# First-layer silu as one ScalarE activation, two more scan pairs on GpSimd, and retimed steps

## The reference, cut to what matters

```python
# x: (16, 512, 256), INNER = 512 channels, 16 states
xx, res = split(x @ in_w.T)                     # 512 channels each
xx = silu(conv4(xx) + conv_b)
delta, B, C = split(xx @ xproj_w.T)             # 16, 16, 16
delta = softplus(delta @ dt_w.T + dt_b)
h[l] = exp(delta[l] * A) * h[l-1] + delta[l] * B[l] * xx[l]    # per channel and state
y[l] = sum over states of h[l] * C[l], + xx * D
x1 = layernorm(x + (y * silu(res)) @ out_w.T)
h = silu((x1 @ w1.T) * w1_s) * ((x1 @ w2.T) * w2_s)            # 1024 wide: the first layer
h = gelu((h @ h1.T) * h1_s)
h = gelu((h @ h2.T) * h2_s)
out = layernorm(x1 + (h @ w3.T) * w3_s)
```

## Time and profile before

| | us |
|---|---|
| median of three runs | 2681.95 (2679.81 to 2683.85) |
| the profiled execution | 2681.34 |
| its span, first to last instruction | 2679.5 |

### The profile page before, as it was taken

The page is one execution under the profiler, slowest core; times in us unless marked ns, Lnnn a source line. Parts: engine busy times, 40 slices in busy tenths (PEclk is TensorE's granted clock), DMA queues, the critical chain, the costliest instruction groups (busy, mean ns, idle before and its releaser), DMA issues. The chain is left out here.

```text
span 2679.5 us, 36236 instructions
## 1 busy us (share of the span) xinstructions
PE 2423.5 (90%) x12098; PEld 1844.0 (69%) x12098; DVE 2413.4 (90%) x2388; ACT 2101.1 (78%) x3225; POOL 1605.8 (60%) x1561
## 2 busy tenths in 40 slices
PE   5677999989999998989999899998989899898988
PEld 2445776867767686776767677686767768576777
DVE  6899999999999999999999999999999999999730
ACT  5886988969788896978879697887969789696611
POOL 1335567665756666566566656656665675657554
PEclk7889999999999999999999999999999999999999
DMA  7758999989899898989989898998989899898933
GB/s 250 217 138 197 223 216 223 228 211 237 206 225 225 214 231 209 238 204 223 223 219 232 206 236 200 228 224 213 243 205 229 204 231 223 212 241 201 254 105 114
DMA packets 224491, 573.26 MB, mean 214 GB/s; under 512 B 25664, under 2 KB 26048, under 8 KB 223824
## 3 DMA queue, kind: packets, MB, share of 16 engines
q0 software_dynamic: 71424, 260.08, 51.9%
q1 hardware_dynamic: 152880, 310.84, 35.3%
HBM read 301.86 MB, written 20.45 MB: 120 GB/s over the span
## 5 line engine op out<-in xcount | busy, mean ns | idle before, releaser
L792 DVE TENSOR_TENSOR_SCAN scan_ps<-dA,scan_ps 128x1024 f32<-128x1024 f32 x411 | 939.7, 2286 | 62.4 <-PE scan_ps L420 61.5
L1001 POOL DMA_DIRECT2D y<-hC x496 | 441.6, 890 | 714.8 <-DVE hC L803 544.6
L651 ACT ACTIVATE dB<-duT,bT 128x512 f32<-128x512 f32 x1024 | 711.0, 712 | 50.9 <-PE scan_ps L420 50.8
L539 PE MATMUL ffn_ps<-hb_hi,ring 128*128 128x512 f32 x1536 | 655.2, 427 | 36.5 <-DVE gate L908 17.4
L642 ACT ACTIVATE dA<-delta,ch 128x512 f32<-128x512 f32 (+1 forms) x1024 | 681.3, 711 | 0.9
L420 PE MATMUL scan_ps<-ident,dB 128*128 128x128 f32 x4096 | 556.7, 282 | 76.8 <-DVE hC L803 60.9
L420 PEld LDWEIGHTS scan_ps<-ident,dB 128*128 128x128 f32 x4096 | 488.1, 145 | 193.7 <-issue 67.2
L539 PE MATMUL ffn_ps<-hb_lo,ring 128*128 128x512 f32 x1536 | 611.2, 398 | 0.0
L803 DVE TENSOR_TENSOR hC<-scan_ps,c_rows_sb 128x1024 f32<-128x1024 f32 x411 | 501.0, 1219 | 42.6 <-DMA c_rows_sb<-c_rows 5.7
L539 PE MATMUL ffn_ps<-ha_hi,ring 128*128 128x512 f32 x1024 | 428.0, 418 | 25.9 <-POOL ha_lo L1042 25.7
L539 PE MATMUL ffn_ps<-ha_lo,ring 128*128 128x512 f32 x1024 | 402.5, 393 | 0.0
(11 more groups left out here) (103 smaller groups left out, 3172.2 us busy)
## 6 DMA issues: line engine op xcount, KB each, us to landing
y<-hC POOLq DMA_DIRECT2D x496, 512.0 KB, 6.3
ring<-rounded_weights SPq DMA_DIRECT2D x704, 256.0 KB, 4.9
c_rows_sb<-c_rows SPq DMA_DIRECT2D x256, 256.0 KB, 5.0
x<-ffn_w SPq DMA_DIRECT2D x22, 512.0 KB, 6.1
rounded_weights<-ffn_w SPq DMA_DIRECT2D x22, 512.0 KB, 6.4
xt<-x_chan SPq DMA_DIRECT2D x16, 512.0 KB, 3.9
xt<-x_tok SPq DMA_DIRECT2D x16, 512.0 KB, 5.5
out_st<-x_chan SPq DMA_DIRECT2D x16, 512.0 KB, 4.9
```

Source lines behind the costliest of these rows:

```text
L539: mm = nc.tensor.matmul(dst, w, a, start=(first and n == 0), stop=(last and n == len(steps) - 1))
L651: nc.scalar.activation(dB[:, n % 2, t, :], duT[:, t, :], ACT.Copy, scale=bT2[:, par, t, n:n + 1]).then_inc(dB_ready, 1)
L792: nc.vector.tensor_tensor_scan(states, dA[:, a:a + 2, :].rearrange("p a l -> p (a l)"), b, 0.0, ALU.mult, ALU.add).then_inc(scan_done, 1)
L1001: pool.dma_start(y2[:, par, c:c + 2, :], hC[:, slot], accum_op=ALU.add).then_inc(y_added[p % 2], 16)
```

## The change

The first layer's activation becomes one Silu on ScalarE with the full scale; VectorE's gate operation goes, and so do the two operations at the start that halved the scales. A PSUM buffer with a first product is now released by ScalarE's silu and no longer by VectorE's gate. Two more pairs of rows 1 to 15, 7 and 10, get their product on GpSimd. Some steps of the tail, the end, the transposes, the first and second layer, the front and the exponentials are a step or two (at most four) earlier or later, and the output's store is issued at step 26 and no longer 24.

```diff
-T_RES = (0, 6, 7, 9)
-T_GATE = (2, 5, 8, 11)
-T_OUT = (12, 14, 16, 17)
+T_RES = (0, 5, 7, 9)
+T_GATE = (2, 5, 8, 10)
+T_OUT = (13, 14, 15, 16)
-E_W3 = (10, 11, 12, 18)
-E_SCALE = (12, 19)
-E_ADD = (14, 20)
-E_STATS = (17, 21)
+E_W3 = (10, 12, 13, 18)
+E_SCALE = (13, 19)
+E_ADD = (15, 20)
+E_STATS = (15, 21)
-L1_AT = (22, 24, 25, 26, 27, 28, 29, 31)
+L1_AT = (23, 24, 25, 26, 27, 28, 30, 31)
-EXP_COUNT = (1, 2, 0, 0, 2, 0, 3, 1, 0, 1, 0, 0, 0, 3, 1, 0, 0, 4, 0, 1, 3, 0, 0, 1, 2, 0, 2, 1, 0, 0, 2, 0, 1, 2,
-             1, 0, 2, 3, 1, 0, 2, 1, 3, 0, 1, 0, 0, 0, 3, 2, 0, 0, 0, 2, 3, 0, 0, 0, 1, 0, 0, 2, 3, 1)
+EXP_COUNT = (0, 3, 0, 0, 2, 0, 1, 2, 2, 0, 0, 2, 1, 2, 1, 0, 0, 0, 2, 1, 4, 0, 0, 0, 3, 1, 0, 1, 0, 2, 1, 0, 1, 0,
+             3, 0, 3, 1, 2, 0, 2, 1, 2, 1, 0, 0, 0, 0, 0, 5, 0, 0, 0, 1, 4, 0, 0, 0, 2, 0, 2, 0, 0, 3)
...
-OUT_AT = 24
+OUT_AT = 26
-POOL_PAIRS = (1, 8, 11, 13, 16, 17)
+POOL_PAIRS = (1, 7, 8, 10, 11, 13, 16, 17)
...
-                        pe.wait_ge(l1_x32 if prev % 2 else l1_gate, f * HC + (prev // 2 + 1))
+                        pe.wait_ge(l1_x32 if prev % 2 else l1_silu, f * HC + (prev // 2 + 1))
...
-                    nc.scalar.activation(gate[:, o % 2, :], ffn_ps[2 * o % 3][:], ACT.Tanh,
-                                         scale=s1_half[:, o:o + 1]).then_inc(l1_tanh, 1)
+                    nc.scalar.activation(gate[:, o % 2, :], ffn_ps[2 * o % 3][:], ACT.Silu,
+                                         scale=fs[:, 0, o:o + 1]).then_inc(l1_silu, 1)
...
-                nc.vector.tensor_scalar(s1_half, s1_half, 0.5, None, ALU.mult).then_inc(const_dve, 1)
...
-                nc.vector.tensor_tensor(s12_half, s1_half, s12_half, ALU.mult).then_inc(const_s12, 1)
...
             def l1_tile(f, o):
-                dve.wait_ge(l1_tanh, f * HC + (o + 1))
-                nc.vector.scalar_tensor_tensor(out=gate[:, o % 2, :], in0=gate[:, o % 2, :], scalar=1.0,
-                                               in1=ffn_ps[2 * o % 3][:], op0=ALU.add, op1=ALU.mult
-                                               ).then_inc(l1_gate, 1)
-                dve.wait_ge(l1_gate, f * HC + (o + 1))
+                dve.wait_ge(l1_silu, f * HC + (o + 1))
                 dve.wait_ge(pe_l1, f * (2 * HC) + (2 * o + 2))
                 if o >= X32:
                     dve.wait_ge(ffn_lo, f * FFN_TILES + (o - X32 + 1))
                 nc.vector.scalar_tensor_tensor(out=x32[:, o % X32, :], in0=gate[:, o % 2, :],
-                                               scalar=s12_half[:, o:o + 1], in1=ffn_ps[(2 * o + 1) % 3][:],
+                                               scalar=fs[:, 1, o:o + 1], in1=ffn_ps[(2 * o + 1) % 3][:],
```

More of the change, by code:

```diff
@@ L47 @@
 T_X1T = (20, 21)
-E_W3 = (10, 11, 12, 18)
-E_SCALE = (12, 19)
-E_ADD = (14, 20)
-E_STATS = (17, 21)
+E_W3 = (10, 12, 13, 18)
+E_SCALE = (13, 19)
+E_ADD = (15, 20)
+E_STATS = (15, 21)
 E_NORM = 22
-B_AT = (-2, 0, 4, 5, 7, 9, 10, 12, 14, 15, 18, 20, 22, 24, 26, 28, 31, 32, 34, 35, 37, 40, 42, 43, 47, 48, 50, 51,
+B_AT = (-2, 0, 3, 5, 7, 8, 10, 12, 14, 15, 18, 20, 22, 25, 26, 28, 31, 32, 34, 35, 37, 40, 41, 42, 47, 48, 50, 51,
         54, 56, 58, 61)
-L1_AT = (22, 24, 25, 26, 27, 28, 29, 31)
+L1_AT = (23, 24, 25, 26, 27, 28, 30, 31)
 L1_SPLIT_AT = (22, 24, 25, 26, 27, 28, 29, 30)
[L57 to L60, removed]
+HALF_AT = (31, 32, 34, 35, 36, 37, 38, 40, 41, 44, 45, 46, 47, 48, 49, 50, 51, 52, 53, 54, 55, 56, 57, 59, 61, 62,
+           63, 66, 67, 70, 71, 72)
+GELU_AT = (38, 39, 39, 45, 47, 47, 49, 50, 56, 57, 57, 65, 65, 66, 72, 73)
+SPLIT_AT = (38, 40, 40, 48, 48, 50, 51, 51, 57, 58, 63, 66, 68, 70, 71, 72)
 F_XX = (30, 32, 34, 36)
@@ L65 @@
 F_BT = 48
[L66 to L75, removed]
+F_BT_OUT = 49
+F_DT = (40, 41, 43, 47)
+F_PLUS = (42, 45, 46, 49)
+F_BASE = (41, 44, 45, 49)
+F_LOST = (45, 47, 49, 51)
+F_LN = 52
+F_DELTA = (54, 54, 54, 54)
+F_DELTA_U = (54, 54, 54, 54)
+F_Y = (55, 56, 60, 62)
+F_DU = (55, 56, 57, 59)
 F_XR = 51
@@ L175, in build @@
         conv_half, a_neg = ch[:, :, 0:TAPS + 1], ch[:, :, C_ALOG:]
-        s1_half, s12_half = fs[:, 0, :], fs[:, 1, :]
         xT_front = xt[:].rearrange("p (k t) d -> p k (t d)", k=KD)
@@ L216, in build @@
         const_conv, const_dve = sem("const_conv"), sem("const_dve")
-        const_exp, const_s12 = sem("const_exp"), sem("const_s12")
+        const_exp = sem("const_exp")
         low_seen_dve, low_seen_act = sem("low_seen_dve"), sem("low_seen_act")
@@ L245, in build @@
         ln_rstd = [sem(f"ln_rstd{i}") for i in range(2)]
-        l1_tanh, l1_gate, l1_x32 = sem("l1_tanh"), sem("l1_gate"), sem("l1_x32")
+        l1_silu, l1_x32 = sem("l1_silu"), sem("l1_x32")
         gelu_x32, ffn_hi, ffn_lo = sem("gelu_x32"), sem("ffn_hi"), sem("ffn_lo")
@@ L252, in build @@
         block = ctx.enter_context(nc.Block())
-        CONST_LOADS, CONST_DVE = 6, 7
+        CONST_LOADS, CONST_DVE = 6, 6
         FFN_TILES = 3 * HC
@@ L775, in scale_constants @@
                                         ).then_inc(const_dve, 1)
-                nc.vector.tensor_scalar(s1_half, s1_half, 0.5, None, ALU.mult).then_inc(const_dve, 1)
                 dve.wait_ge(const_exp, 1)
                 nc.vector.tensor_scalar(a_neg, a_neg, -1.0, None, ALU.mult).then_inc(const_dve, 1)
-                dve.wait_ge(const_dve, CONST_DVE)
-                nc.vector.tensor_tensor(s12_half, s1_half, s12_half, ALU.mult).then_inc(const_s12, 1)
             def scan_pair(r, p):
```

## The result

The changed kernel takes 2754.3 us (median of four runs, 2752.2 to 2755.3) beside 2680.9 for the kernel before: a ratio of 1.0272, with an interval of 1.0259 to 1.0285. It is 73 us slower; 2688 was forecast, in a range that ended at 2745.

The account below looks back on a forecast made before the run. Each row was taken as some 110 us set by TensorE's queue and 47 by VectorE. Pairs -1.2 and -0.8, first layer +2.6, taken as +0.5 a row; with the last stretch, 2681.3 + 6.8 = 2688 us, range 2600 to 2745.

Parts of the forecast that it names:

- Two stretches, one set by TensorE, one by VectorE.: Each row: some 110 us set by TensorE's ordered queue, some 47 us (normalisation, first layer, first convolution taps) set by VectorE.
- The table loads.: Silu on ScalarE needs its own table loads (72 in 100), ten a row, each adding 1.42 us to the queue.
- The chain in the first layer.: ScalarE's silus, exponentials, scales and eight loads take 25.9 us and become the chain; the stage is 2.6 us longer.
- The two pairs.: Products of pairs 7 and 10 moved to GpSimd shorten each row's VectorE-set stretch by 1.2 and 0.8 us.
- Most lie in TensorE's stretch, where they move waits and no work.: Other moved steps counted at nothing; bounds, together with doubt on the loads, -3.8 to +3.8 us a row.
- Rival 1: First layer: silu shares Exp's table, no loads; GpSimd's splits come next; 4.5 us a row gained, 2613 us; chance 0.28.
- Rival 2: First layer: TensorE's new pauses bring the lower clock for the whole stage, some 5 us a row, 2760 us; chance 0.10.
- The sign named for this case: TensorE waiting in its long stretch would show that the moved steps and not the silu made the time.

Follow-up runs that it names:

- the run that took it back: Changed kernel with the front's last delta product on TensorE put back from step 47 to 46, all else kept: 2721.7 us, ratio 1.0142.
- The gate alone: Kernel before with VectorE's gate operation removed and one Tanh left, needing no added table load; steps and pairs kept: 2655.6 us, ratio 0.9907.
- the kernel with the single number: Kernel before with only the front's last delta product on TensorE moved from step 46 to 47: 2732.4 us, ratio 1.0187.

## Why the prediction was wrong, point by point

- **Two stretches, one set by TensorE, one by VectorE.** This held as a picture of the kernel before, and misled where it was turned into a rule: that hardly anybody waits in the long stretch does not mean that nothing there can be made to wait.
- **The table loads.** Right. The counts were 76 and 75 more (some 75 each were forecast), 348 in all, and a load costs 1.41 us on the queue (dB at 1222.34 and silu at 1224.36 us are 2.02 apart, against 0.61). The Trainium skill's larger figure for a switch, 2.66 us with a drain (ScalarE: Activation LUTs, "What ACT_TABLE_LOAD costs"), weighed in the prediction, is not borne out by these 1.41 us.
- **The chain in the first layer.** Right: 25.9 us from the first silu to the eighth, ScalarE without idle time, VectorE waiting 7.9 us for it in a row, the scan of step 32 29.5 us after the first silu's start (29.6 forecast). The stage by itself is +3.2 us against +2.6.
- **The two pairs.** Half-sized: 0.9 us a row and not 2.0 when made alone. That 1.2 and 0.8 us come through failed: ScalarE's copy and exponentials were next late. In the changed kernel, where the first layer's first product also moved from step 22 to 23, steps 8 to 23 gained 1.9; that this is near the 2.0 of the sum is luck, since the moved steps have a share in it. For steps 8 to 31 together the sum gave +0.6 and the trace +1.3.
- **"Most lie in TensorE's stretch, where they move waits and no work."** This is the step that failed. The moved steps were taken at nothing, with 3.8 us a row as the bound on either side; in the changed kernel steps 32 to 63 and 0 to 7 are 3.5 us a row longer. Over fifteen rows that is 52 us, and nearly two thirds of it is one number: 33 us, by the run that took it back. The bound came from the size of the waits that existed and not from the room that each moved instruction had before its consumers and before what stands behind it in its engine's list. What moved was work: 1.05 us of TensorE's, from ahead of two groups of transposes to between them. VectorE waits 1.30 us for the second group, its next two operations meet GpSimd's and stretch by 2.7, and the next scan is 4.0 us late. In the kernel before, the same number makes TensorE wait as well, 1.37 us for the Relu. Both were to be read from the code: the place of the product in TensorE's list, and the transposes in step 48, which need all four Relus, the last of them moved from 47 to 48.
- **Rival 1** (no load) had the wrong next wait in the kernel as it was: without the gate alone VectorE waits for ScalarE's convolution activation and TensorE; GpSimd's split is the late one only with the changed steps (2.0 us in the row shown). The gate alone gave 25 us, below the 2.5 us a row (38 us) allowed for.
- **Rival 2** (the lower clock through the first layer) did not happen: the granted clock was 1.00 in that stage. It fell in steps 48 to 55 instead (0.93); with the silu alone, in the steps of before, it was 0.94 in the first layer.

The range's upper end, 2745, stood for +4.3 us a row (0.5 and 3.8); the row took +4.9 (1.3 and 3.5). The sign named for this case, waits of TensorE in its long stretch, is what the trace shows, 2.14 us at a split in steps 48 to 55, but as the last link: VectorE's wait for TensorE comes ahead of it.

What stays open: the 1.2 us in steps 0 to 7 that are left when the one number is taken back. They leave with the front's steps as a group, but that group makes only 0.5 us there in the kernel before. In these steps ScalarE makes ten exponentials where the kernel before makes 7.5, and VectorE waits 2.6 us for its gate activations. Which of the moved steps does this was not separated.

## What to carry to other kernels

When a step is moved later, list who needs its result and in which step they stand, and what now stands behind it in the list of its own engine, with who waits for that. If the room falls to nothing, price the wait, everything queued behind it, and the operations it pushes beside another engine's. An activation with a table of its own has to be grouped if it is to pay for the VectorE work that it saves: here ten loads a row lost 53 us in the steps of before. With four a row and the two pairs, the kernels measured lie between 11 us behind and 21 us ahead; the pairs gave 14 by themselves, so, if the two add, at best some 7 us are left for the grouped silu. No run has it without the pairs. A bound on moving things in a stretch can't be read from the waits that it has.

## What the runs showed of the hardware

**VectorE's small operations wait for GpSimd's.** Durations of the plus-one (min, median, max in ns) in the kernel before:

```profile
L838 DVE TENSOR_SCALAR out_st<-du x32: 413/429/1334, 33.6 to 2360.6; 128x512 f32<-128x512 f32 x32
```

and in the one with a single number changed:

```profile
L838 DVE TENSOR_SCALAR out_st<-du x32: 414/1216/2169, 34.7 to 2403.1; 128x512 f32<-128x512 f32 x32
```

Sorted by what GpSimd did at the same time, all 64 plus-ones of each kernel: with nothing or only a DMA issue on GpSimd beside them they took 408 to 429 ns (49 cases in the two kernels), with a two-input GpSimd operation up to 2169 (79 cases). It is a wait and no slower pace: in 72 of the 79 the GpSimd operation was under way first, and the plus-one ended 0.28 to 0.30 us after it, whatever was left of it; in six the plus-one started 0.11 to 0.14 us ahead and took 426 or 427 ns. In the remaining one, the longest, it started 0.31 us ahead and waited all the same. In the kernel after, the plus-one of step 49 met two operations in turn, a product (1293.03 us) and a one-input cast (1294.27), and ended 0.29 us after the cast. The products with C (line 803), which read one operand from PSUM, don't show it: in the kernel before 1186 to 1227 ns in the 227 cases with such an operation beside them, 1204 to 1226 in the 184 without. The Trainium skill says that VectorE and GpSimd share one pair of ports to SBUF, that it is locked for a whole instruction, and that VectorE needs it in its two-port modes or with two inputs from SBUF (SBUF — State Buffer, "SBUF: two separate sides"); the trace agrees, with these numbers. So a late operation on VectorE can cost more than its lateness: here 1.3 us of waiting became 4.0.

**The granted clock after a pause.** In the kernel with the single number, TensorE stood for 1.37 us and then made the transposes; the second layer's products behind them start 0.43 us apart, and from 1279.42 us on 0.23: the levels of 1.2 and 2.4 GHz, as in the earlier trace rows. The mean granted clock from the transposes' start to there is 0.60. Its timeline there:

```profile
1276.92 0.63 PE L539 MATMUL ffn_ps<-ha_lo,ring 128*128 128x512 f32 x1
1277.35 0.63 PE L539 MATMUL ffn_ps<-ha_hi,ring 128*128 128x512 f32 x1
...
1279.42 0.39 PE L539 MATMUL ffn_ps<-ha_lo,ring 128*128 128x512 f32 x1
1279.64 0.39 PE L539 MATMUL ffn_ps<-ha_hi,ring 128*128 128x512 f32 x1
```

So a wait of TensorE in its long stretch costs again in the products behind it. In the kernel after the pause comes later, at the split (1305.85 us), and the stage's granted clock is 0.93 there too.
